# Layer 3 of a four-layer network: from one batch after another to a written-out pipeline over three batches

## What is computed

```
zxbcdt = x @ W_in.T                       # z 512 | xBC 768 | dt 64
xBC = silu(causal_conv4(xBC))             # 6 channel groups of 128
dt = softplus(dt_raw + dt_bias); a = dt * -exp(A_log)
cum = cumsum(a); L = exp(cum_i - cum_j) for j <= i
CB = C @ B.T ; M = CB * L * dt            # 64 heads of width 8, one B and C for all
y = M @ xs + D * xs                       # and the same across chunks of 128
y = y * silu(z); y = y * rsqrt(mean(y*y)) * norm_w ; out = y @ W_out.T
ffn(x) = (sigmoid(x @ Q(w1).T) * (x @ Q(w2).T)) @ Q(w3).T    # Q ternary, width 704: 6 pieces
```

## Time and profile before

| | us |
|---|---|
| median of three runs | 1151.35 |
| the profiled execution, whole | 1151.5 |
| its span, first to last instruction | 1149.7 |
| layer 3 in it, from its first instruction to the end | 679.7 to 1149.7 |
| period of one batch in layer 3 (first turn L2260 at 686.1, fourth at 1034.1) | 116.0 |

### The profile page before, as it was taken

The page is one execution under the profiler, slowest core; times in us unless marked ns, Lnnn a source line. Parts: engine busy times, 40 slices in busy tenths (PEclk is TensorE's granted clock), DMA queues, the critical chain, the costliest instruction groups (busy, mean ns, idle before and its releaser), DMA issues. The chain is left out here.

```text
span 1149.7 us, 13089 instructions
## 1 busy us (share of the span) xinstructions
PE 969.4 (84%) x4130; PEld 500.7 (44%) x4130; DVE 815.7 (71%) x1432; ACT 449.7 (39%) x732; POOL 463.9 (40%) x480
## 2 busy tenths in 40 slices
PE   3888859979999999579999959888988898889777
PEld 1555535523333333235565545325533553355324
DVE  3667655578888786447768737796679767967795
ACT  1111124427766666257536424311442134224421
POOL 2111047555444442025426420681068206910681
PEclk9999979969999999779999978899889988998899
DMA  8500006322222210020000010000000000000000
GB/s 299 181 14 14 14 0 167 109 64 57 57 67 60 70 30 1 25 107 14 1 15 15 1 39 1 1 1 1 18 0 0 0 18 0 0 9 9 0 0 18
DMA packets 28635, 42.95 MB, mean 37 GB/s; under 512 B 6480, under 2 KB 21792, under 8 KB 28192
## 3 DMA queue, kind: packets, MB, share of 16 engines
q1 hardware_dynamic: 28592, 42.41, 11.9%
HBM read 30.93 MB, written 11.27 MB: 37 GB/s over the span
## 5 line engine op out<-in xcount | busy, mean ns | idle before, releaser
L991 DVE TENSOR_REDUCE l_nmax<-banks 128x1 f32<-128x512 f32 (+1 forms) x165 | 147.9, 930 | 35.0 <-PE banks L1094 34.1
L2328 PE MATMUL banks<-l_scaled,l_cbm 128*128 128x512 f32 x224 | 126.9, 687 | 44.1 <-POOL l_scaled L2038 21.2
L950 ACT ACTIVATE l1b_PT<-banks 128x512 f32<-128x512 f32 (+1 forms) x176 | 134.1, 793 | 67.0 <-PE banks L1107 66.6
L2038 POOL TENSOR_TENSOR l_scaled<-l_X,l_source 128x512 f32<-128x512 f32 x112 | 132.6, 1210 | 0.0
L2207 DVE TENSOR_TENSOR banks<-banks,l_decay 128x512 f32<-128x512 f32 x128 | 87.9, 689 | 18.0 <-PE banks L2328 11.0
L2328 PEld LDWEIGHTS banks<-l_scaled,l_cbm 128*128 128x128 f32 x224 | 41.8, 210 | 116.2 <-POOL l_scaled L2038 76.1
L1094 PE MATMUL banks<-l_KQ 96*128 96x512 bf16 x240 | 82.0, 395 | 7.9 <-DVE l_nmax L991 5.0
L1107 PE MATMUL banks<-l_KQ 99*128 99x512 bf16 x256 | 85.7, 388 | 2.8 <-ACT l1b_PT L950 2.1
L2181 DVE TENSOR_TENSOR l_y<-l_y,banks 128x512 f32<-128x512 f32 x128 | 86.5, 676 | 1.9
L2107 ACT ACTIVATE l_hhi<-l_h 128x512 f16<-128x512 f32 (+1 forms) x24 | 15.1, 630 | 144.5 <-DVE l_h L2220 144.5
L1121 PE MATMUL banks<-l1b_PT,l1b_V 128*32 128x512 f32 x512 | 68.2, 605 | 0.0
(11 more groups left out here) (326 smaller groups left out, 2083.6 us busy)
## 6 DMA issues: line engine op xcount, KB each, us to landing
l_split<-l1a_parts SPq DMA_DIRECT2D x16, 384.0 KB, 3.7
l_KQ<-l_split SPq DMA_DIRECT2D x48, 128.0 KB, 2.9
l_KQ<-l_split SPq DMA_DIRECT2D x16, 192.0 KB, 3.0
l_KQ<-l_split SPq DMA_DIRECT2D x48, 64.0 KB, 2.9
w_ternary<-l_tern_out SPq DMA_DIRECT2D x7, 384.0 KB, 2.3
x<-in_x SPq DMA_DIRECT2D x4, 512.0 KB, 9.5
l_raw<-in_w_gate_up SPq DMA_DIRECT2D x2, 1024.0 KB, 10.0
out<-x SPq DMA_DIRECT2D x4, 512.0 KB, 3.0
```

What stands on the lines that cost most here:

```text
L950: nc.scalar.activation(PT[:, first:first + size, :], source, ACT.Exp, scale=SCALE).then_inc(p_ready, 1)
L991: nc.vector.tensor_reduce(nmax[:, H % 2, first:first + size], source, axis=AX.X, op=ALU.max, negate=True).then_inc(smax_read, 1)
L2038: nc.gpsimd.tensor_tensor(by_head(scaled[:, n % 4, :]), by_head(X[:, T, :]), spread(source[:, level, T, :]), ALU.mult).then_inc(scaled_rea ...
L2328: last = nc.tensor.matmul(bank, cbm[:, T % 2, level, :], scaled[:, own_n % 4, :], start=True, stop=True)
```

## The change

In layer 1 the memset of KQ moves behind POOL's second power. In layer 3 the loops over batches are written out for b = -1 to 4. One unit is one level of two tiles (tiles 0 and 1 for units 0 to 6, tiles 2 and 3 for units 7 to 13, then one unit across 128 and one across 256): 16 units, or slots, in a batch, in two pairs of banks in turn (banks 4 and 5, 6 and 7). Slot by slot, the beginning of batch b + 1 and the end of batch b - 1 are laid between the units of batch b. These use banks 2 and 3 alone, the feed-forward's first half banks 0 and 1. POOL multiplies X by dt once (instead of the decays by dt on DVE), masks CB for tiles 2 and 3, and forms C*B, from which PE gets the diagonal. ACT normalises x, and also y, so that the down and output products add up in PSUM and one addition to x is left for two tiles. The diff, cut to its core (helpers that only rename an old instruction are left out):

```diff
-            nc.gpsimd.memset(early.KQ[ROWS:ROWS + PARTS, KEY, :, :, :], 1.0).then_inc(early.ones_set, 1)
-            pool.wait_ge(early.ones_set, 1)
             invert(0)
             for b in range(B):
                 add_bias(b)
                 if b + 1 < B:
                     invert(b + 1)
+                if b == 0:
+                    pool.wait_ge(rstd_ready, 2)
+                    nc.gpsimd.memset(early.KQ[ROWS:ROWS + PARTS, KEY, :, :, :], 1.0).then_inc(early.ones_set, 1)
...
+    UNITS = 2 * LEVELS + 2
+    OWN = 2 * LEVELS
+    C_BANK = (2, 3, 2, 3, 2, 3)
+    def unit_bank(u):
+        return 4 + 2 * (u % 2)
...
+            def start(b, half):
+                mine = slice(2 * half, 2 * half + 2)
+                pool.wait_ge(coef_ready, b + 1)
+                pool.wait_ge(xtok_ready, b * TT + 2 * half + 2)
+                nc.gpsimd.tensor_tensor(by_head(y[:, b % 2, mine, :]), by_head(X[:, b % 2, mine, :]), spread(coef[:, mine, :]),
+                                        ALU.mult).then_inc(y_started, 1)
+                pool.wait_ge(y_started, b * 2 + half + 1)
+                nc.gpsimd.tensor_tensor(by_head(X[:, b % 2, mine, :]), by_head(X[:, b % 2, mine, :]), spread(dt[:, mine, :]),
+                                        ALU.mult).then_inc(xdt_ready, 1)
+            def scale(b, n):
+                ...
+                if q >= 2:
+                    pool.wait_ge(prod_made, own_unit(q - 2) + 1)
+                nc.gpsimd.tensor_tensor(by_head(scaled[:, n % 2, :, :]), by_head(X[:, b % 2, mine, :]),
+                                        spread(decay[:, b % 2, level, mine, :]), ALU.mult).then_inc(scaled_ready, 1)
...
+            for b in range(-1, B):          # POOL
+                if b >= 0:
+                    for n in range(OWN):
+                        scale(b, n)
+                        if n == 0 and b:
+                            rest_of_gated(b - 1, 2)
+                            rest_of_gated(b - 1, 3)
+                        if n == 1 and b:
+                            rest_of_gated(b - 1, 4)
+                        if n == 2:
+                            rest_of_input(b)
+                            if b:
+                                invert_rms(b - 1)
+                        if n == 3 and b:
+                            rest_of_gated(b - 1, 5)
+                        if n == 4:
+                            start(b, 1)
+                        if n == 5:
+                            mask_late(b, 2)
+                            mask_late(b, 3)
+                        if n == 10:
+                            scale_across(b, 0)
+                            scale_across(b, 1)
+                        if n == 12 and b + 1 < B:
+                            multiply_states(b + 1)
+                    rest_of_gated(b, 0)
+                else:
+                    multiply_states(0)
+                if b + 1 < B:
+                    start(b + 1, 0)
+                if b >= 0:
+                    rest_of_gated(b, 1)
+                if b + 2 < B:
+                    invert(b + 2)
+            for j in range(2, FT):
+                rest_of_gated(B - 1, j)
+            invert_rms(B - 1)
...
+                for u in range(UNITS):      # DVE
+                    if u == 13 and ahead:
+                        weigh_skip(b + 1)
+                    if now and u >= 12:
+                        multiply_gate(b, u - 12)
+                    if behind and u < 2:
+                        multiply_gate(b - 1, u + 4)
+                    if behind and u in (9, 10):
+                        add_x(b - 1, u - 9)
+                    if now:
+                        apply_decay(b, u)
+                    if now and u:
+                        add(b, u - 1)
+                    elif behind and u == 0:
+                        add(b - 1, UNITS - 1)
+                    if behind and u == 0:
+                        gate_y(b - 1, 0)
+                        gate_y(b - 1, 1)
+                    if u == 1 and behind:
+                        mean_square(b - 1)
+                    if u == 2 and ahead:
+                        copy_turned(b + 1)
+                    if u == 3:
+                        if ahead:
+                            take_steps(b + 1)
+                    if ahead and 4 <= u < 8:
+                        softplus(b + 1, u - 4)
+                    if ahead and 4 <= u < 4 + XBC:
+                        convolve(b + 1, u - 4)
+                    if u == 11 and b + 2 < B:
+                        statistics(b + 2)
+                    if u == 15 and b + 2 < B:
+                        shifts(b + 2)
+                    if u == 14 and ahead:
+                        mask(b + 1, 0)
+                        mask(b + 1, 1)
...
+            def product(b, u):              # PE
+                g = b * UNITS + u
+                if g >= 2:
+                    pe.wait_ge(prod_added, g - 1)
+                ...
+                    for i in range(2):
+                        last = nc.tensor.matmul(ps[bank + i][:, :], cbm[:, 2 * (u // LEVELS) + i, u % LEVELS, :],
+                                                scaled[:, u % 2, i, :], start=True, stop=True)
+                for u in range(UNITS):
+                    if now:
+                        product(b, u)
+                    if now and u < 2:
+                        gates(b, 2 * u)
+                        gates(b, 2 * u + 1)
+                    if behind and u == 0:
+                        feed_forward(b - 1, FT - 1)
+                    if u == 2:
+                        if now:
+                            late_states(b)
+                        if ahead:
+                            turn_input(b + 1)
+                    if u == 3:
+                        if ahead:
+                            steps(b + 1)
+                    if behind and u == 4:
+                        turn_y(b - 1)
+                    if ahead and 3 <= u < 3 + XBC:
+                        channels(b + 1, u - 3)
+                    if behind and 5 <= u < 5 + TT:
+                        project(b - 1, u - 5)
+                    if ahead and u in (8, 9):
+                        sums(b + 1, 2 * (u - 8))
+                        sums(b + 1, 2 * (u - 8) + 1)
+                    if ahead and u == 10:
+                        sums(b + 1, 4)
+                    if ahead and u == 12:
+                        sum_states(b + 1)
+                        turn_tokens(b + 1, 0)
+                    if ahead and u == 13:
+                        for t in range(1, TT):
+                            turn_tokens(b + 1, t)
+                    if ahead and u == 13:
+                        states(b + 1, 0)
+                        states(b + 1, 1)
+                    if now and u >= 11:
+                        feed_forward(b, u - 11)
```

More of the change, by code:

```diff
@@ L2068, in _, with normalise @@
[L2068 to L2070 removed]
+            def normalise(b):
+                act.wait_ge(shift_ready, b + 1)
+                if b:
+                    act.wait_ge(xt_made, b * CT)
+                for t in range(TT):
+                    last = nc.scalar.activation(xn[:, t, :], k.x[:, b, t, :], ACT.Identity, bias=shift[:, t:t + 1],
+                                                scale=rstd[:, t:t + 1])
+                last.then_inc(xn_ready, 1)
@@ L2275, in _ @@
-                width = TT * L3_HEADS
-                pe.wait_ge(dt_read, b + 1)
-                pe.wait_ge(c_read, b * XBC + 2)
-                pe.wait_ge(a_ready, b + 1)
-                flat = lambda bank, first: bank[:, first:first + width].rearrange("p (t h) -> p t h", t=TT)
-                for level in range(LEVELS):
-                    nc.tensor.matmul(ps[level // 2][:, (level % 2) * width:(level % 2 + 1) * width], w.sums[:, level, :],
-                                     a[:, :, :].rearrange("p t h -> p (t h)"), start=True, stop=True)
@@ L2283, in _ @@
-                out = flat(ps[L128 // 2], (L128 % 2) * width)
-                for T in range(TT):
-                    last = nc.tensor.matmul(out[:, T, :], w.sums[:, PREFIX if T % 2 else SUFFIX, :], a[:, T, :],
-                                            start=True, stop=True)
-                last.then_inc(sums_made, 1)
-                pe.wait_ge(c_read, b * XBC + 3)
-                out = flat(ps[4], 0)
-                for T, kind, more in ((0, SUFFIX, 1), (1, SUFFIX, None), (2, PREFIX, None), (3, PREFIX, 2)):
-                    last = nc.tensor.matmul(out[:, T, :], w.sums[:, kind, :], a[:, T, :], start=True, stop=(more is None))
-                    if more is not None:
-                        last = nc.tensor.matmul(out[:, T, :], k.ones[:, :], a[:, more, :], start=False, stop=True)
@@ L2345, in _ @@
-                pe.wait_ge(h_ready, b * FT + FT)
-                pe.wait_ge(hsplit, b * FT + FT)
-                pe.wait_ge(down_loaded, 16)
-                for t in range(TT):
-                    for j in range(FT):
```

(33 more changed lines are left out.)

723 lines of the change are left out of this document (441 added, 282 removed).

## The result

The changed kernel takes 1160.99 us (median of 5, 1159.70 to 1162.59), the kernel before 1150.13 beside it: 1.0105 times as long, 95% interval 1.0062 to 1.0147. It is slower by 11 us. The forecast was 1151.0, no change; the time lies in its range, but the kernel moved, and the interval excludes no change. The profiled execution took 1162.59, with a span of 1160.8.

What follows compares the result with a forecast made beforehand. Layer 3's stages wait for one another, two engines overlapping only in the products. 733.6 + 357 + 25.5 - 1.9 + 39.8 = 1154.0, less 4.8, plus 1.8 around the span: 1151 us, no change; forecast range 1130 to 1172, wider range 1113 to 1177.

Steps and rivals of the forecast that it cites:

- gates of y: Layer 3, VectorE's gating of y: collisions with GpSimd there add 1.5 us in each of three batches.
- a clock that starts low: Layer 3's batches: 3 us added to the slot times for PE's low clock at the start.
- closed round of 4.5 us: Layer 3: product(u + 1) waits for add(u - 1), queued behind apply_decay(u), which waits for product(u); at least 4.5 us a unit.
- rival C: Layer 3: banks are free earlier, so no closed round; light slots 3.5 us, batch 3 68, time 1133; chance 0.05.
- the list of slots without them: Layer 3: lengths of a middle batch's slots 0 to 15 without any collision, 4.5 to 8.5 us each, 94 us together.
- no engine over its share: Layer 3: no engine's work per batch exceeds 116 us; PE leads with 84, DVE 73, POOL 59.
- Rivals A and B: Layer 3: A, collisions hardly count, 1112 to 1130, chance 0.31; B, DVE and POOL in lock step, from 1175 up, 0.19.
- The term 53.9: Layer 3's first beginning, up to the first product: 53.9 us, +5.9 against 48.0; bounds +1 and +10.
- the 4.8 us: Layer 1: gain from moving the memset that ran beside L104, -4.8 us; bounds -4.8 and 0.
- the sum of 25.5: Layer 3's DVE and POOL collisions: 9 us in batch 0, 12 in batches 1 and 2, 4.5 for gates of y.
- PE waiting for ACT ... which I take as covered: Layer 3: ACT, with some 45 us of work a batch, was taken not to hold PE up; no time counted.
- GpSimd's 6.3 and 5.9 at units 4 and 5: Layer 3, batch 3: POOL's work of 6.3 and 5.9 us binds at units 4 and 5, in a batch of 79.

Runs made afterwards that it cites:

- e7: Changed kernel with 8, 5 and 6 useless matmuls 128x512 in TensorE's idle time before the last layer's first product; 1155.07 us.
- e1: Changed kernel with VectorE adding each unit to y right behind its own decay, in the same slot instead of one later; 1135.24 us.
- e5: Changed kernel with GpSimd's start of y and second-half X scaling moved from slot 4 to 1, two late masks from slot 5 to 3; 1152.71 us.
- e4: Changed kernel with the second layer's memset of ones back at its old place, ahead of everything else on GpSimd; 1163.66 us.
- e14: Changed kernel with 8 useless matmuls 128x256 on TensorE ahead of the second layer's first turning; 1155.53 us.
- e10: Changed kernel with 20 useless matmuls 128x256 on TensorE ahead of the second layer's first turning; 1162.22 us.
- e13: Changed kernel with ACT gating z of tiles 0 and 1 and rounding the input before the previous batch's last sigmoid and first two squares; 1165.91 us.

## Why the prediction was wrong

The forecast was no change, the difference of gains and losses of some 45 us each. The span came out at 1160.8 where the sum has 1149.2, 11.6 us more. Set term by term against the sum (us; 101.5 is 94 + 6 + 1.5, and 76.6 is 79 + 1.5 less the 1.9 and the 2.0 at its two ends):

| | sum | measured | more |
|---|---|---|---|
| start of the last layer | 674.9 | 676.7 | 1.8 |
| its beginning, up to the first product | 53.9 | 56.5 | 2.6 |
| first product up to the first decay | 2.0 | 3.8 | 1.8 |
| batch 0, collisions in it | 96 | 96.2 | 0.2 |
| batches 1 and 2, with collisions and gates of y | 2 x 101.5 | 103.9 + 104.3 | 5.2 |
| batch 3, up to the last decay | 76.6 | 79.9 | 3.3 |
| a clock that starts low | 3 | in the rows above | -3 |
| from the last product to the end | 39.8 | 39.5 | -0.3 |

- **What held.** The closed round of 4.5 us (4.4 in several slots of each batch; rival C is out), the rule for collisions, the list of slots without them, the last end, no engine over its share. Rivals A and B are out: the collisions cost 20.9 to 26.3 us, and a middle batch takes 104 us, not 94 or 110. The Trainium skill, "SBUF — State Buffer", section "Who interferes with whom", says that a VectorE instruction with two SBUF inputs contends with a GpSimd instruction that reads SBUF, under one rule of an exclusive lock; its words "fully blocks", which the prediction quotes, stand there with VectorE's 2-port modes. The runs agree with the rule: 5.61 us for three instructions that take 2.32 alone.
- **The step that failed is the price of the clock**: "3 us for a clock that starts low". It measured about 8.9. (1) The first beginning and its product, 2.6 + 1.8. The term 53.9 was built on the 48.0 us of the kernel before, at a clock of 0.78; the changed kernel's stood at 0.68. That it is the clock shows e7, which gets 5.9 us back, more than these 4.4. (2) The last batch, for which the sum has no clock at all: slots 9 and 10 took 5.5 and 6.2 instead of 4.5, and the windows of slots 8 to 11 show where the clock fell:

```profile
1085.14:1090.19 5.05, 5.01 (x24) 3.00 (x22) 2.95 (x3) 0.00 (x0) 3.57 (x2) 1.00 0.00 0
1090.19:1095.64 5.45, 3.00 (x4) 0.82 (x4) 2.95 (x3) 0.00 (x0) 4.20 (x3) 0.80 0.29 95
1095.64:1101.87 6.23, 3.82 (x5) 1.48 (x6) 2.35 (x3) 0.00 (x0) 1.96 (x1) 0.50 0.01 3
1101.87:1106.30 4.43, 4.43 (x13) 1.68 (x12) 3.04 (x4) 1.23 (x2) 2.22 (x2) 0.80 0.01 2
```

  PE had little more than a product to do in slots 9 and 10 (4 or 5 records, after 24 in the slot before), stood idle for 2.44 us ahead of each, and the clock went to its lower level, 1.2 of 2.4 GHz; the two products then took 3.0 and 3.8 us instead of 1.9, all of it in a closed round. With the round open (e1) the last batch ran at 1.00. In e5, whose round is closed too but whose clock fell later (1.00 in slot 9, 0.84 in slot 10), the same slots took 4.4 and 5.2. About 2.7 us; this is read from traces and not from a run of its own. (3) The second layer: of the 4.8 us, 3.0 arrived in the profile (1.8 missing) and 2.7 in the times (e4). L104 fell to 0.17 us as forecast and the turning came 4.9 us sooner, but the first values (VectorE's first write of l_values) only 0.9 sooner, at 171.0 for 172.0:

```profile
146.58 0.17 DVE L104 TENSOR_SCALAR l1a_rstd<-l1a_mv 128x4 f32<-128x4 f32 x1
```

  The clock did not come up sooner with the earlier turning, but later: from 160 to 165 us PE was busy 5.00 of 5.00 us in both kernels, at 0.83 in the kernel before and 0.50 in the changed one. From the turning to the first values it took 16.6 us before, 20.6 in the changed kernel, and 14.0 in e14, which had the full clock all the way. (The expectation of e10 says that the low clock stayed until 165 in both; that was misread.) How the rest of the 3.0 us was won behind the first values no run shows.

  Together 1.8 + 2.6 + 1.8 + 2.7 = 8.9 where 3 were counted: 5.9 of the 11.6 us.
- **The collisions of the middle batches were under-priced.** Slots 4 to 9 took 49.1 and 49.2 us where the list and its 6 us give 47.0: 8.1 and 8.2 for 6, together 4.3 of the 11.6 us. That the sum of 25.5 came out is partly luck. It held another 4.5 for the gates of y, which cost next to nothing (slot 1 is 6.9 with whole and 6.7 with tiny scalings, and slot 0 is as long as PE's list).
- **"PE waiting for ACT ... which I take as covered."** In slot 1 of two batches it isn't: 6.9 us against 5.2.

```profile
841.80 3.70 PE L2595 MATMUL banks<-w_inner,l_xnT 128*128 128x512 f32 x8 [1.45 <-ACT l_z L2152]
```

  4.1 us in the last three batches, hidden in the total by the 4.5 for the gates of y, which lie in the same slots. A busy sum of 42 us in 104 says nothing of an order in which z stands behind a sigmoid and two squares. That the wait is there is shown; that it can be had back is not (e13).
- **The rest**, 1.4 us, was not taken apart. In the last batch GpSimd's 6.3 and 5.9 at units 4 and 5 didn't come (4.7 and 5.1).

## What to carry to other kernels

When two engines each wait tens of microseconds for the other and neither is full, look for a release that stands one instruction too late in a queue: here adding a unit behind its own decay gave 26 us. A written order must also say beside what each step runs: GpSimd's scaling left a decay that reads PSUM at 1.23 us and stretched three convolution steps from 2.32 to 3.9 us, two scalings to 5.61. A mean that falls in one group (the convolution in e1) can have risen in another, so take the engine's whole busy time. And price TensorE's low clock wherever it idles on the path, at the end of a pipeline too; a few matmuls of no use ahead of real ones gave 5 to 6 us twice, 20 of them where 8 fit gave nothing (1162.2 for 1161.0).

## What the runs showed of the hardware

- A wait that is shortened ahead of a cold TensorE gives back only part: the memset's move gave 4.9 us at the turning and 0.9 us at the first values (171.0 for 172.0). The low clock stood for 6.3 us behind the turning in the kernel before (155.4 to 161.7) and for 14.6 us in the changed one (150.4 to 165.0). Eight matmuls of no use, with the turning at the same moment, brought the first values to 164.7.
- The same code came through the window from 150 to 170 us with a clock of 0.62 or 0.90, and its last layer then started at 678.0 or 673.4: a profile against a profile has some 4 us of scatter here, more than the medians have.
- Less GpSimd work doesn't always mean a shorter stretch: with scalings of 64 columns it was 363.4 us, with half scalings 358.0, though VectorE was busy 259.1 us in the first and 266.2 in the second.
- Opening the round moved the meetings of VectorE and GpSimd and did not lessen them: 292.9 us of VectorE work in the stretch for 289.1, with the convolution's mean down from 1.18 to 0.93 us.
